# A decoder megakernel: the wide attention's mask moved to VectorE, expert and recurrent stage ends merged

## What is computed

```
layer 0: a0 self attention, 16 heads of 8   | x0 cross attention, 16 heads | ffn0: 8 experts, hidden 512, silu gate
layer 1: a1 paged self attention with rope  | x1 cross attention           | ffn1: 1 expert, hidden 384, silu gate
layer 2: selective state-space recurrence   | x2 cross attention, 2 masks  | ffn2: 8 experts, hidden 256, relu, Sinkhorn router
layer 3: a3 self attention                  | x3 "wide": 16 heads of 64    | ffn3: 8 experts, hidden 256, bias

scores = q @ k.T * scale;  scores = where(mask == 0, scores, NEG)
p = softmax(scores);       out = (p @ v) @ Wo
expert:  y = (silu(x @ Wg) * (x @ Wu)) @ Wd;   x += coef[:, e] * y   (all experts are computed)
recurrence's last step:  r = layernorm(y @ out_proj) * gamma + beta;  x += r
```

## Time and profile before

| | us |
|---|---|
| median of 3 runs | 2431.86 (2429.22 to 2435.39) |
| the profiled execution: its time | 2440.75 |
| the profiled execution: its span | 2438.9 |
| TensorE busy | 2066.0 (85%) |
| VectorE busy | 1662.4 (68%) |
| ScalarE busy | 1045.7 (43%) |
| GpSimd busy | 533.2 (22%) |

### The profile page before, as it was taken

One profiled execution on the slowest core, in us unless ns is written; L12 is line 12 of the kernel. 1 busy time (PEld: TensorE's weight loads), 2 busy tenths in 40 slices (PEclk: granted clock), 3 DMA queues, 4 the chain that ended last, 5 costly groups with the idle time before them and its releaser, 6 DMA issues. The chain is left out here.

```text
span 2438.9 us, 36556 instructions
## 1 busy us (share of the span) xinstructions
PE 2066.0 (85%) x12192; PEld 1383.0 (57%) x12216; DVE 1662.4 (68%) x4273; ACT 1045.7 (43%) x2326; POOL 533.2 (22%) x905
## 2 busy tenths in 40 slices
PE   6698899998999897767774997598699979999888
PEld 3455788884555455433332554587334348777777
DVE  5666677786675576779997565456679856666655
ACT  2354222222564453455551344322367734444333
POOL 0342110102110530068883321010211010000010
PEclk8698899997897799889996798799689979999989
DMA  8321000004120420000003220000511110000000
GB/s 338 99 60 23 1 1 1 1 1 130 44 53 18 121 60 2 1 1 0 1 1 105 73 48 8 1 1 1 174 36 46 33 44 1 1 1 1 1 1 18
DMA packets 60073, 94.61 MB, mean 39 GB/s; under 512 B 11313, under 2 KB 33137, under 8 KB 58737
## 3 DMA queue, kind: packets, MB, share of 16 engines
q1 hardware_dynamic: 29312, 55.29, 6.7%
q0 software_dynamic: 29952, 36.45, 6.2%
q10 hardware_dynamic: 624, 0.54, 0.1%
HBM read 65.50 MB, written 31.29 MB: 40 GB/s over the span
## 5 line engine op out<-in xcount | busy, mean ns | idle before, releaser
L1008 DVE TENSOR_REDUCE m<-banks 128x1 f32<-128x512 f32 (+3 forms) x512 | 272.6, 584 | 94.6 <-PE banks L1172 54.4
L2687 PEld LDWEIGHTS banks<-w_ffn,eh 128*128 128x128 f32 x2144 | 279.2, 191 | 23.5 <-DVE eh L2628 1.9
L2687 PE MATMUL banks<-w_ffn,eh 128*128 128x128 f32 x2144 | 281.2, 274 | 1.5 <-DVE eh L2628 1.5
L1140 ACT ACTIVATE p<-banks 128x512 f32<-128x512 f32 (+3 forms) x512 | 234.0, 522 | 101.4 <-PE banks L1218 58.7
L1443 DVE TENSOR_REDUCE m<-banks 128x2 f32<-128x308 f32 x384 | 165.7, 475 | 137.1 <-PE banks L1743 70.3
L2675 PE MATMUL banks<-x_hi,w_hi 128*128 128x512 f32 x472 | 211.2, 447 | 17.4 <-PEq L332 17.4
L1170 PE MATMUL banks<-K,Qf 32*128 32x512 f32 (+2 forms) x512 | 182.5, 515 | 14.6 <-PEq L332 9.9
L2657 ACT ACTIVATE et<-banks 128x512 f32<-128x512 f32 x140 | 83.6, 597 | 246.8 <-PE banks L2677 203.2
L2677 PE MATMUL banks<-x_hi,w_lo 128*128 128x512 f32 x472 | 188.7, 400 | 0.0
L2676 PE MATMUL banks<-x_lo,w_hi 128*128 128x512 f32 x472 | 187.6, 397 | 0.0
L1216 PE MATMUL banks<-Q,K 32*128 32x512 f32 (+2 forms) x512 | 153.5, 499 | 14.9 <-ACT p L1140 13.0
(11 more groups left out here) (423 smaller groups left out, 4332.7 us busy)
## 6 DMA issues: line engine op xcount, KB each, us to landing
Qf<-stack_q_plain POOLq DMA_DIRECT2D x48, 256.0 KB, 3.0
Qf<-stack_q_masked POOLq DMA_DIRECT2D x32, 256.0 KB, 3.0
K<-stack_k_self POOLq DMA_DIRECT2D x32, 256.0 KB, 3.1
w_ffn<-ffn_dram SPq DMA_DIRECT2D x1, 6144.0 KB, 35.2
stack_q_plain<-q_hi SPq DMA_DIRECT2D x24, 256.0 KB, 3.1
stack_q_masked<-q_hi SPq DMA_DIRECT2D x16, 256.0 KB, 3.0
stack_k_self<-k_hi SPq DMA_DIRECT2D x16, 256.0 KB, 3.8
K<-stack_k_ctx POOLq DMA_DIRECT2D x48, 80.0 KB, 2.7
```

Of the source, the lines that this page charges most:

```text
L1008: ins = dve.reduce_max(k.m[:, t, h:h + 1], bank[:, 0:(t + 1) * P if k.kind == "page" else S], AX)
L1140: nc.scalar.activation(k.p[:, x % PBUFS, q0:S], score_banks[x % 3][:, q0:S], ACT.Exp).then_inc(sem("exp_done"), 1)
L2687: last = pe.matmul(bank[:, t * P:(t + 1) * P], k.h[:, n % RING, t * P:(t + 1) * P], w(down.format(e))[:, i * P:(i + 1) * P], start=(i == 0 ...
```

## The change

**The wide attention.** The two bf16 mask matmuls of a step are gone. VectorE forms mask x NEG + bank in one operation for each of the two banks and writes it to a new SBUF tile `s` (128 x 308 each); the maxima are taken from `s`, and ScalarE's exponentials read `s`. The scores of step n wait for the two new operations of step n-2 in place of its exponentials; the wait for prT stays.

```diff
-                    pe.wait_ge(sem("exp_done"), GROUP * (n - 1))
+                    pe.wait_ge(sem("mask_ready"), 2 * (n - 1))
                     pe.wait_ge(sem("prT_ready"), n - 1)
...
             def maxima(n):
+                if n >= 2:
+                    dve.wait_ge(sem("exp_done"), GROUP * (n - 1))
                 for i in range(2):
                     dve.wait_ge(sem("scores_done"), 2 * n + i + 1)
-                    last = dve.reduce_max(k.m[:, n % 2, i::2], ps[2 * (n % 2) + i][:, 0:2 * S2]..., AX)
+                    dve.scalar_tensor_tensor(k.s[:, n % 2, i], over(k.mq[:, t, 0:S2], 1, 2), NEG, own, ALU.mult, ALU.add)
+                for i in range(2):
+                    dve.wait_ge(sem("mask_ready"), 2 * n + i + 1)
+                    last = dve.reduce_max(k.m[:, n % 2, i::2], k.s[:, n % 2, i], AX)
```

```diff
+                pe.matmul(y_bank[:], k.d_hi[:, at], h_hi, start=i == 0, stop=False)
+                pe.matmul(y_bank[:], k.d_lo[:, at], h_hi, start=False, stop=False)
+                pe.matmul(y_bank[:], k.d_hi[:, at], h_lo, start=False, stop=i == tiles - 1).then_inc(sem("h_used"), 1)
...
+                nc.gpsimd.tensor_tensor(k.h_lo[:, n % HRING], k.h[:, n % RING], k.h_hi[:, n % HRING].bitcast(F32), ALU.subtract)
...
+                nc.scalar.copy(k.h_hi[:, n % HRING], k.h[:, n % RING]).then_inc(sem("h_high"), 1)
```

```diff
-    apart = experts - min(experts, 2) if ahead else experts
+    apart = max(0, experts - k.rings + 1) if ahead or store else experts
...
-        experts(None, None, "silu", ("L1_w", "L1_d"), 1, 3, norm_kind="one", ahead=2)
+        experts(None, None, "silu", ("L1_w", "L1_d"), 1, 3, rings=1, norm_kind="one", ahead=2)
...
-        experts("f2_router", route_sinkhorn, "relu", ("w{}", "d{}"), E8, 2, keep_x=True, norm_kind="double", ahead=2)
+        experts("f2_router", route_sinkhorn, "relu", ("w{}", "d{}"), E8, 2, rings=4, keep_x=True, norm_kind="double", ahead=2)
...
+            for b in range(B):
+                sp.wait_ge(sem("x_added"), pairs.index((experts - 1, b)) + 1)
+                sp.dma_start(out[:, b * QT:(b + 1) * QT, :], x_of(net, b)).then_inc(stored, 16)
```

```diff
             def add_scanned(b):
+                ch.link(dve.tensor_tensor(tiles, tiles, over(w("m_gamma"), 1, QT), ALU.mult))
+                dve.wait_ge(sem("with_offset"), b + 1)
+                ch.link(dve.tensor_tensor(x, x, tiles, ALU.add))
...
                 maximum(c)
+                if c < PIECES:
+                    vector_norm_piece(dve, ch, net.x, k.n, (B - 1) * QT, B * QT, c)
```

More of the change, by code:

```diff
@@ L2160, in scores @@
                     out = ps[2 * (n % 2) + j % 2][:, j // 2 * S2:(j // 2 + 1) * S2]
-                    pe.matmul(out, k.qT[rows, c, t * P:(t + 1) * P], k.kk[rows, c, 0:S2], start=j < 2, stop=False, skip_group_check=True)
-                for i in range(2):
-                    out = ps[2 * (n % 2) + i][:, 0:2 * S2].rearrange("p (h k) -> p h k", h=2)
-                    pe.matmul(out, w("negi"), over(k.mq[:, t, 0:S2], 1, 2), start=False, stop=True, skip_group_check=True).then_inc(sem("scores_done"), 1)
+                    last = pe.matmul(out, k.qT[rows, c, t * P:(t + 1) * P], k.kk[rows, c, 0:S2], start=j < 2, stop=j >= 2, skip_group_check=True)
+                    if j >= 2:
+                        last.then_inc(sem("scores_done"), 1)
             def turn(n):
@@ L2323, with __init__ @@
 class Router:
-    def __init__(self, net, sb):
+    def __init__(self, net, sb, rows):
         n = QT * B
@@ new lines, in cut_weight @@
+def cut_weight(net, pool, k, name, e, i, before):
+    width = k.kinds * P
+    n, done = (e * k.tiles + i) % k.wring, before + i + 1
+    src = net.w(name.format(e))[:, i * width:(i + 1) * width]
+    if e >= k.rings:
+        pool.wait_ge(net.sem("h_ready"), ((e - k.rings + 1) * B - 1) * k.tiles + i + 1)
+    pool.tensor_copy(k.w_hi[:, n], src).then_inc(net.sem("w_hi_ready"), 1)
+    pool.wait_ge(net.sem("w_hi_ready"), done)
+    pool.tensor_tensor(k.w_lo[:, n], src, k.w_hi[:, n].bitcast(F32), ALU.subtract).then_inc(net.sem("w_ready"), 1)
+    pool.wait_ge(net.sem("w_ready"), done)
@@ L2564, in experts_block, with cut_down @@
-def experts_block(net, k, act_kind, names, experts, tiles, norm_kind=None, ahead=0):
+        cut_weight(net, pool, k, name, e, i, before)
+def cut_down(net, pool, k, name, e, i):
+    n, done = (e * k.tiles + i) % k.wring, e * k.tiles + i + 1
+    src = net.w(name.format(e))[:, i * P:(i + 1) * P]
+    if e >= k.rings:
+        pool.wait_ge(net.sem("h_used"), ((e - k.rings + 1) * B - 1) * k.tiles + i + 1)
+    pool.tensor_copy(k.d_hi[:, n], src).then_inc(net.sem("d_hi_ready"), 1)
+    pool.wait_ge(net.sem("d_hi_ready"), done)
+    pool.tensor_tensor(k.d_lo[:, n], src, k.d_hi[:, n].bitcast(F32), ALU.subtract).then_inc(net.sem("d_ready"), 1)
+    pool.wait_ge(net.sem("d_ready"), done)
@@ L2572, in experts_block @@
+def experts_block(net, k, act_kind, names, experts, tiles, norm_kind=None, ahead=0, store=None):
+    nc, sem, ps, w = net.nc, net.sem, net.ps, net.w
+    first, down = names
+    apart = max(0, experts - k.rings + 1) if ahead or store else experts
     pairs = [(e, b) for e in range(apart) for b in range(B)]
@@ L2695, in _ @@
                     output(n - 2)
+        @block.sync
+        def _(sp):
+            if store is None:
+                return
+            out, stored = store
+            for b in range(B):
+                sp.wait_ge(sem("x_added"), pairs.index((experts - 1, b)) + 1)
+                sp.dma_start(out[:, b * QT:(b + 1) * QT, :], x_of(net, b)).then_inc(stored, 16)
+            sp.wait_ge(stored, 16 * B)
     net.normed = ahead
@@ L3155, in narrow_attention, with cross_attention, experts @@
                 narrow_block(net, k, pre)
-        def cross_attention(pre, kind):
+        def cross_attention(pre, kind, finish=False):
             stack, sb = scope()
             with stack:
-                cross_block(net, Cross(net, sb, kind), pre, 1.0 / float(np.sqrt(np.float32(HD))))
+                cross_block(net, Cross(net, sb, kind), pre, 1.0 / float(np.sqrt(np.float32(HD))), finish)
         class One:
             pass
-        def experts(weight, route, act_kind, names, n, tiles, keep_x=False, norm_kind=None, ahead=0):
+        def experts(weight, route, act_kind, names, n, tiles, rings=3, keep_x=False, norm_kind=None, ahead=0, store=None):
             stack, sb = scope()
@@ L3173, in experts @@
                     route(net, r)
-                experts_block(net, e, act_kind, names, n, tiles, norm_kind, ahead)
+                if turned:
+                    turned_block(net, e, names, n, tiles, ahead)
+                else:
+                    experts_block(net, e, act_kind, names, n, tiles, norm_kind, ahead, store)
         stack, sb = scope()
@@ L3199, in program @@
         wait_loaded("ffn0")
-        experts("f0_router", route_mean, "silu", ("w{}", "d{}"), E8, 4, norm_kind="one", ahead=3)
+        experts("f0_router", route_mean, "silu", ("w{}", "d{}"), E8, 4, rings=2, ahead=3)
         ffn0_room.close()
@@ L3252, in program @@
         wait_loaded("ffn3")
-        experts("f3_router", route_tokens, "bias", ("w{}", "o{}"), E8, 2)
+        experts("f3_router", route_tokens, "bias", ("w{}", "o{}"), E8, 2, store=(ov, stored))
         with nc.Block() as block:
```

255 lines of the change are left out of this document (198 added, 57 removed).

## The result

The changed kernel takes 2464.0 us (median of 4 runs, 2460.5 to 2477.3) against 2433.6 us (2429.2 to 2436.9): ratio 1.0127, 95% interval 1.0103 to 1.0152, so +31 us, between 25 and 37. The profiled execution has a span of 2460.4 us, 21.5 more than that of before. The forecast was +17, and 2449 us.

What follows compares the result with a forecast made beforehand. It took a loop between TensorE and VectorE to bound the wide stage. Terms 23 - 3.5 - 4.8 + 6.2 + 3.7 - 5.5 - 2 = +17 us gave 2449 against the median 2431.86; range 2424 to 2465.

Steps and rivals of the forecast that it cites:

- the clock's term: Wide stage: nothing in the sum; a clock falling from 0.95 with TensorE's longer idle times was a sign of being wrong.
- ffn0: First expert stage: -3.5 us, from -9 for the projection's steps, +1.9 for the tail and +3.5 for norm pieces.
- The wide loop: Wide attention: TensorE and VectorE wait in turn; a plain step goes from 3.08 to 3.63 us, +23 us for the stage.
- The steps that project outputs: Wide attention: three or so steps a batch, 3.8 to 4.7 us each and TensorE's, would change by 0.
- ffn1: Expert stage: two norms instead of one behind a last hidden tile that is 1.1 us earlier, +3.7 us.
- The small terms: Stage by stage: x1 +3.7 us, ffn2 -5.5, ffn3 -2, ffn1 +3.7, x2 with the finish -4.8.
- the +2.5: x0: batch 3's norm stands between the first maxima, while the norm of twelve tiles before the first scores becomes shorter, +2.5 us.
- +8.5: x2: added prelude work, GpSimd's blocking and delayed batch 3, taken off a start 13.3 us earlier, leaving -4.8 us.
- TensorE as the bound of the wide stage: First rival, wide attention: mask work fits VectorE's spare 114 us, 18 us go, 2408 us; chance 0.12.
- The low part of ffn0: Second rival, ffn0: GpSimd's low part is late and stalls TensorE 0.12 us a step, +15 for -3.5, 2467 us; chance 0.10.
- ffn0's full gain: Third rival, ffn0: transposes overlap, so it gains 20 us more than forecast, 2429 us; chance 0.12.
- a finish that is hidden whole: Fourth rival: x2's prelude hides the finish whole (-13.3) and wide steps cost half (+12), 2431 to 2441 us; chance 0.12.

Runs made afterwards that it cites:

- d: Kernel before, with VectorE copying prT ahead of pT in the wide attention: ratio 0.9955 to the kernel before, -11 us.
- e: Kernel before, with the wide attention's two mask matmuls left out and no mask applied: plain step 2.81 us, wide stage 311.7 us.
- j: Kernel before, with the change's wide attention part and prT copied ahead of pT: plain steps 3.10 us, wide stage 337.0 us.
- f: Kernel before with the change's wide part, but mask operation writing back to its bank, read by maxima and exponentials: plain steps 3.65 us, wide stage 344.3 us.
- c: Changed kernel with the wide attention of before put back: ratio 1.0008 to the kernel before, +2 us; wide stage 320.8 us.
- g: Changed kernel with ffn1's order of before (norm pieces from step 5 on): ratio 1.0092 to the kernel before.
- i: Kernel before, with only ffn1's norm pieces put behind its last hidden step: ratio 1.0019 to the kernel before, +4.6 us.
- h: Changed kernel without its wide part, norms of x0 and x1 whole, ffn1 as before, prT copied first: ratio 0.9939 to the kernel before, -15 us.
- l: Same as h, but norms of x0's batches 1 to 3 in one go of twelve tiles: ratio 0.9917 to the kernel before, 2413.6 us.

## Why the prediction fell short

The direction, the loop in the wide attention and most of the prices were right; the size was not, +31 us for +17. The step that failed is the clock's term, which the sum has at nothing. Every price was taken at the clock of the one profile of before, and the fall of the clock stands only among the signs of being wrong. That sign came: in the wide stage the clock is 0.92 to 0.93 in the four profiles of its new code, where it was 0.95 to 0.97 in the four of the old. What it cost is worked out below: some 4 us in the wide stage (an estimate) and 3.4 us in the recurrence, a stage for which the prediction has no term at all. The remaining 5 us between the table's two sums are mostly the unchanged stages (+4.2) and x0 (+1.3), less what ffn0 gained beyond its forecast (-1.7). Point by point:

**The wide loop** was read rightly: 3.63 forecast for a plain step, 3.64 measured, first mask operation 0.87 us after the scores (0.8 forecast). d, e and j confirm the loop from three sides. One reading in its working is wrong: 1.04 ns a column is not "VectorE's own pace in 686 less 343", which is 343 ns for 384 columns, 0.89 each. The conclusion drawn from it, no discount for memory, was right all the same (f). The 504 ns for a mask operation came from that flatter line and was too much: it measured 471. The term of 0.80 for two came out near (0.78 from the first one's start to the maxima's), because the overlap taken off each of them, about 0.1, was too much as well (0.08): two errors that in part cancel.

What the sum missed is at a batch's start. Steps are counted here from one negated maximum to the next. Windows over the second and third such interval of the second batch, before

```profile
2078.55:2083.80 5.25, 3.47 (x20) 2.82 (x21) 1.92 (x5) 2.25 (x13) 0.59 (x2) 0.69 0.00 0
2083.80:2089.35 5.55, 5.55 (x27) 4.81 (x26) 3.31 (x12) 1.59 (x8) 0.29 (x1) 0.50 0.00 0
```

and after:

```profile
2083.42:2089.00 5.58, 4.46 (x20) 3.68 (x21) 2.68 (x8) 1.95 (x10) 0.59 (x2) 0.50 0.00 0
2089.00:2094.34 5.34, 5.34 (x26) 4.64 (x25) 3.97 (x13) 1.74 (x8) 0.29 (x1) 0.50 0.01 2
```

A batch's first steps run partly at the lower clock (0.50 is 1.2 GHz). Before, that varies from batch to batch; after, it holds in most batches for the better part of two intervals. Over four profiles of the old stage and four of the new, 16 batches each, the first four intervals of a batch sum to 13.7 and 15.9 us (+2.3), with mean clocks of 0.82 and 0.80 in the second and third before, 0.54 and 0.67 after. The eleven behind them sum to 40.3 and 44.9 (+4.6). Together 6.9 x 4 = 28; the stage's start (+0.9) and its end (-0.4) nearly cancel.

How much of that is clock can be told from intervals at like clocks. The second interval, in the kernel c with the old stage and in the changed kernel, with almost the same busy time of TensorE:

```profile
2077.62:2083.19 5.57, 3.88 (x20) 3.07 (x21) 1.93 (x6) 2.26 (x13) 0.59 (x2) 0.59 0.00 0
2254.66:2259.78 5.12, 3.90 (x20) 3.28 (x21) 2.68 (x8) 1.95 (x10) 0.59 (x2) 0.63 0.00 0
```

and the third at the full clock, in c and in g:

```profile
2161.49:2164.89 3.40, 3.30 (x30) 2.92 (x28) 3.21 (x11) 1.59 (x8) 0.29 (x1) 1.00 0.00 0
2255.93:2260.16 4.23, 3.92 (x32) 3.36 (x31) 3.97 (x13) 1.74 (x8) 0.29 (x1) 1.00 0.00 0
```

At like clocks the four intervals change by +0.7 (1.02 to 1.74), -0.45, +0.83 and +0.56 (3.08 to 3.64), 1.7 in all, and the eleven at the full clock by +4.2. That is 5.9 a batch, where the prediction has 6: at an unchanged clock its +23 to 24 was right, and so was its +0.3 for the first step of a batch (+0.7 and -0.45). The other 0.6 and 0.4 a batch, some 4 us in the stage, go with the lower clock. This split is an estimate from these rows. That TensorE's longer wait at a batch's start (first negated maxima 1.73 apart, before 1.02) is what lowers the clock is likely by i, which showed it in ffn1; for the wide batches it was not tested.

**The steps that project outputs**, forecast at 0, cost 0.2 each (4.68 to 4.90). In f, one profile, it was 4.75, so most of that seems to come with reading `s`.

**ffn1** was right in its own stage, and wrong in stopping there. The two norms stand in a row behind the last hidden tile, as VectorE's timeline has it (answering to the earlier trace rows):

```profile
979.99 0.86 DVE L392 BATCH_NORM_STATS2 stats<-x 128x6 f32<-128x128 f32 x4
...
984.90 0.87 DVE L392 BATCH_NORM_STATS2 stats<-x 128x6 f32<-128x128 f32 x4
...
989.82 0.69 DVE L2844 TENSOR_TENSOR x<-x,banks 128x512 f32<-128x512 f32 x1
```

The pieces behind the last hidden step leave TensorE idle for longer, and the recurrence, which nobody touched, starts at 0.69 instead of 0.75: +3.4 in the mean, shown by g and i.

**The base.** The first profile's wide stage, 324.3 us, is the longest of four of that code (318.3 to 324.3, 320.9 in the mean without the hand-over). Against it the changed stage's 349.2 is +25, and the agreement with the forecast +23 would have been luck; against the mean it is +28. The profiled execution was one draw, and the prediction took its stages as the kernel's.

**The small terms**: x1, ffn2, ffn3, ffn1 and x2 were right within 0.6 (the final wait of SyncE is 1.9 us now). In x1 TensorE now waits 2.19 us for the norm of batch 3, as forecast. ffn0 gained 5.2 for 3.5. Its steps are 2.21 us apart in the mean, the forecast's figure, made of about 2.16 up to the last two experts and 2.36 in them, where the norm pieces stand; the tail behind the last step grew by 3.9 us for the 1.9 of the working. Its steps without a turned output come out at 2.04 us, nine matmuls from one L2766 to the next but one, for the 2.06 of the working:

```profile
341.14 0.39 PE L2766 MATMUL banks<-x_hi,w_hi 128*128 128x512 f32 x1
...
343.18 0.39 PE L2766 MATMUL banks<-x_hi,w_hi 128*128 128x512 f32 x1
```

GpSimd's low part was in time, at 1298 ns each:

```profile
L2664 POOL TENSOR_TENSOR h_lo<-eh,h_hi 128x512 fp32r<-128x512 f32 x128 | 164.9, 1298 | 60.3 <-ACT h_hi L2728 57.1
L2781 PE MATMUL banks<-h_hi,d_hi 128*128 128x512 f32 x128 | 53.0, 414 | 2.6 <-POOL h_lo L2664 2.0 <-issue 0.6
```

TensorE waited for it 2.0 us in the whole stage. In x0 the +2.5 (measured +3.8) had the wrong reason: it charges the pieces behind the maxima and credits the shorter norm ahead of the scores, but by h and l the loss is the same without the pieces, and is gone with one norm of twelve tiles. That GpSimd's additions hold up VectorE's small operations in x2 came as written:

```profile
1319.28 1.12 DVE L374 TENSOR_SCALAR rstd<-bits 128x4 int32<-128x4 int32 x1
1320.43 1.01 DVE L376 TENSOR_TENSOR sq<-rstd 128x4 f32<-128x4 f32 x1
1321.48 1.01 DVE L377 TENSOR_TENSOR sq<-sq,vh 128x4 f32<-128x4 f32 x1
...
1340.01 0.48 DVE L1448 TENSOR_REDUCE m<-banks 128x2 f32<-128x308 f32 x1
```

Three operations of 0.17 us took 1.0 to 1.1 each beside GpSimd's. The first maximum came 34.9 us after x2's start where it came 23.8 after it, +11.1, while that start moved 13.3 us nearer to the scan's end. The forecast has +8.5 for the prelude and the late norm of batch 3 together; the prelude alone took more, and some 2 us came back behind the first maximum, so the -4.8 came out well by two errors that cancel. The operations of ffn0 that read a bank kept their 686 ns (685 for L2700) beside a GpSimd that is busy for three quarters of the stage. The Trainium skill (SBUF — State Buffer, Who interferes with whom) spares a VectorE instruction with at most one SBUF input only outside the modes in which it takes both ports, a condition that the prediction left out. It matters here: L374 reads one SBUF tile and took 1.12 us. With the condition in place the Trainium skill does not contradict these rows.

**The rivals.** TensorE as the bound of the wide stage fell with d and e. The low part of ffn0 was not late, and neither ffn0's full gain nor a finish that is hidden whole came.

## What to carry to other kernels

Where two engines hand a buffer to each other, find the loop and price the edit in it; shares of busy time said that VectorE had 114 us to spare, and work moved there cost 0.83 us a step against the 0.27 it saved. Then look at what stands in the loop for no reason: the exchange of two copies gained 11 us by the times (6.6 by the stage's means), more than any part of the change. A stage that begins after TensorE has waited is a draw of the clock, so take its time from several profiles, and when an edit lengthens TensorE's wait at the end of one stage, add the start of the next one to its price.

## What the runs showed of the hardware

The granted clock at a stage's start differs between executions of the same kernel, and moves the recurrence's first part by 5 us (64.7 or 69.6), the wide stage by 6 (318.3 to 324.3) and a1's attention, which no edit touched, by 9 (203.5 to 212.7). A longer wait of TensorE at the end of the stage before shifts the odds (10.5 us for 5.5: 68.0 to 69.5 in five kernels of five). A maximum of 308 elements takes VectorE 464 ns from memory and 470 to 474 from a PSUM bank, so the source is no reason to move one; for ScalarE's exponentials of 154 elements memory is the slower source, 414 ns against 389.
